# One stretch of scores and one of value products per sequence in a two-layer attention and FFN kernel

## What is computed

```python
h = shift_token(x)
q, k, v = split(h @ wqkv)
q, k = rotary_xpos(l2norm(q) * qs, l2norm(k) * ksc)
x = x + local_attention(q, k, v) @ wo
h = layernorm(shift_token(x)) * lg + lb
a, g = split(h @ w1 + b1)
x = x + (a * gelu(g)) @ w2 + b2
```

## Time and profile before

| | |
|---|---|
| median of 3 runs | 1419.7 us (1419.18 to 1420.46) |
| profiled execution, span | 1416.2 us (3.5 us below the median; its own device time isn't listed) |
| TensorE busy | 1385.3 us |
| VectorE busy | 1090.6 us |
| ScalarE busy | 935.8 us |
| GpSimd busy | 761.9 us |

### The profile page before, as it was taken

The page is one execution under the profiler, slowest core; times in us unless marked ns, Lnnn a source line. Parts: engine busy times, 40 slices in busy tenths (PEclk is TensorE's granted clock), DMA queues, the critical chain, the costliest instruction groups (busy, mean ns, idle before and its releaser), DMA issues.

```text
span 1416.2 us, 32735 instructions
## 1 busy us (share of the span) xinstructions
PE 1385.3 (98%) x11563; PEld 1237.8 (87%) x11563; DVE 1090.6 (77%) x3067; ACT 935.8 (66%) x2662; POOL 761.9 (54%) x576
## 2 busy tenths in 40 slices
PE   8999999989999999999999999999999999999998
PEld 7999998778888888888888888888888888888887
DVE  5777776768788788888888878778778888888874
ACT  6877777456666666666666667666666666666662
POOL 1212222556566566666666667666656666666653
PEclk9999999999999999999999999999999999999999
DMA  5223122101100100010001211111111111111001
GB/s 190 90 92 110 48 67 90 47 20 29 30 30 30 30 29 28 28 28 28 28 29 29 71 29 37 33 35 37 37 37 37 36 36 36 36 36 37 29 30 31
DMA packets 50516, 63.41 MB, mean 45 GB/s; under 512 B 8402, under 2 KB 32104, under 8 KB 50408
## 3 DMA queue, kind: packets, MB, share of 16 engines
q1 hardware_dynamic: 50408, 61.99, 14.0%
HBM read 38.17 MB, written 16.78 MB: 39 GB/s over the span
## 4 chain that ended last, share of the span: by engine, by line
PE 65%; DVE 16%; ACT 9%; issue 5%; DMA 2%; POOL 1%; SPq 1%; DVEq 0%; ACTq 0%; POOLq 0%
PE pb L567 30%; PE pb L880 6%; PE pb L894 6%; PE pb L856 5%; PE pb L825 5%; PE pb L840 5%; ACT x_p L1079 4%; PE pb L920 4%; DVE p_t L1596 2%; DVE p_t L1610 2%; ACT x_pt L1085 2%; DVE r_sin L1583 2%; DVE n_sq L1562 2%; DMA x<-x 1%; DVE r_cos L1577 1%
## 5 line engine op out<-in xcount | busy, mean ns | idle before, releaser
L1823 POOL TENSOR_TENSOR n_inv<-n_cl,half_neg 128x16 f32<-128x16 f32 x64 | 211.2, 3299 | 178.2 <-DVE n_cl L1567 174.7
L1222 ACT ACTIVATE p_t<-p_t,s_nm 128x128 f32<-128x128 f32 (+1 forms) x512 | 227.0, 447 | 22.3 <-DVE s_nm L1596 20.9
L567 PE MATMUL pb<-h_hi,w_hi 128*128 128x256 f32 x704 | 207.5, 295 | 1.3 <-DVE h_lo L1558 1.2
L567 PE MATMUL pb<-h_hi,w_lo 128*128 128x256 f32 x704 | 198.7, 282 | 0.0
L567 PE MATMUL pb<-h_lo,w_hi 128*128 128x256 f32 x704 | 198.6, 282 | 0.0
L1828 POOL TENSOR_TENSOR r_cos<-r_cos,r_sin 128x1024 f32<-128x1024 f32 x64 | 154.6, 2415 | 53.8 <-DVE r_sin L1583 53.8
L1213 ACT ACTIVATE pt_t<-pb 128x512 f32<-128x512 f32 x192 | 114.3, 597 | 98.5 <-PE pb L840 97.8
L1178 ACT ACTIVATE qk_sq<-pb 128x512 f32<-128x512 f32 x128 | 72.5, 592 | 142.9 <-PE pb L567 141.5
L567 PE MATMUL pb<-wqkv_hi,xt_hi 128*128 128x512 f32 x384 | 163.9, 427 | 2.6 <-DVE r_sin L1583 2.3
L1859 POOL TENSOR_TENSOR hg_lo<-hg,hg_hi 128x256 fp32r<-128x256 f32 (+1 forms) x192 | 141.9, 760 | 44.5 <-DVE hg_hi L1627 44.5
L1596 DVE CUSTOM_DVE_ANT_0 p_t<-pb,mask_t 128x128 f32<-128x128 f32 (+1 forms) x512 | 151.9, 353 | 17.5 <-PE pb L825 17.3
(11 more groups left out here) (145 smaller groups left out, 3907.5 us busy)
## 6 DMA issues: line engine op xcount, KB each, us to landing
y_state<-x SPq DMA_DIRECT2D x32, 256.0 KB, 2.0
x_cur<-y_state SPq DMA_DIRECT2D x32, 256.0 KB, 2.6
x_res<-y_state SPq DMA_DIRECT2D x32, 256.0 KB, 2.8
x_in<-x SPq DMA_DIRECT2D x16, 256.0 KB, 2.9
x_state<-x SPq DMA_DIRECT2D x16, 256.0 KB, 2.0
x_orig<-x_state SPq DMA_DIRECT2D x16, 256.0 KB, 2.9
out<-x SPq DMA_DIRECT2D x16, 256.0 KB, 2.2
x<-x SPq DMA_DIRECT2D x32, 112.0 KB, 2.3
```

The costliest lines, as they stand in the source:

```text
L567: mm = pe.matmul(dst, s, m, start=(n == 0 and k == 0), stop=(n == len(pairs) - 1 and k == 2))
L1222: e = nc.scalar.activation(pu, pu, ACT.Exp, bias=s_nm[:, j, k:k + 1], scale=-1.0, accum_out=s_sum[:, j, k:k + 1])
L1823: nc.gpsimd.tensor_tensor(n_inv[:, t], n_cl[:, t], half_neg[:], ALU.pow).then_inc(pool_inv, 1)
```

## The change

The first pair of units now has window 0 (128 keys, four heads each); pairs 1 and 2 have window 1. Each unit has a bank of its own (2, 7, 3, 5, 4, 6), and all three pairs of scores stand at the head of the iteration. Pair 2 waits for the first residual, which reads bank 6; `feed(0)`, which writes bank 7, waits for the maxima of unit 1. All value products of an item are one stretch behind `turn_p(5)`, and wait for all six copies. The copies write into `p_t`, and `pt_t` is gone. On ScalarE `exps(0)` stands ahead of the squares. The orders of VectorE and GpSimd are the same, but unit numbers mean other heads: `maxes`, `exps`, `inverse_sums` and `norm_probs` have four heads of 128 keys in units 0 and 1 and two of 256 keys in units 2 to 5. The core of the diff (the same new arguments at other calls and the idle products of iteration 1 are left out):

```diff
-        pt_t = sb("pt_t", [P, 4, 512], where=L)
...
-        S_BANK = [3, 4, 3, 4, 3, 4]
+        S_BANK = [2, 7, 3, 5, 4, 6]
...
+        def keys_of(u):
+            return P if u < 2 else T
+
         def heads_of(u):
 
-            return range(u // 2 * 4 + u % 2, u // 2 * 4 + 4, 2) if u < 4 else range(u % 2, HEADS, 2)
+            return range(u % 2, HEADS, 2) if u < 2 else range((u // 2 - 1) * 4 + u % 2, u // 2 * 4, 2)
...
                         pe.wait_ge(act_qkt, at(plus(a, -1), 4, 3 if part == 1 else 4))
+                        if part == 2:
+                            pe.wait_ge(dve_max, at(plus(a, -1), UNITS, 1))
...
-                    pe.wait_ge(dve_max, at(b, UNITS, 5))
+                    pe.wait_ge(dve_max, at(b, UNITS, 3))
...
-                        pe.wait_ge(dve_max, at(b, UNITS, UNITS))
+                        pe.wait_ge(dve_max, at(b, UNITS, 5))
...
-            def scores(a, b, j):
+            def scores(a, b, c, j):
 
                 if j == 0:
                         pe.wait_ge(act_qkt, at(b, 4, 4))
+                    if c is not None:
+                        pe.wait_ge(dve_olo, at(c, 2, 2))
+                elif j == 1:
                     if a is not None:
                         pe.wait_ge(act_xhi, at(a, 1, 1))
                         pe.wait_ge(dve_xlo, at(a, 1, 1))
-                else:
-                    pe.wait_ge(dve_max, at(b, UNITS, 2 * j))
-                win1 = j < 2
-                keys = T if win1 else P
-                q_cols = slice(P, T) if win1 else slice(0, P)
+                elif c is not None:
+                    pe.wait_ge(dve_x1, at(c, 1, 1))
+                keys = keys_of(2 * j)
+                q_cols = slice(P, T) if j else slice(0, P)
...
                 pe.wait_ge(dve_pn, at(b, UNITS, u + 1))
+                if u == 0:
+                    pe.wait_ge(dve_max, at(b, UNITS, 4))
...
-            def weigh(b, c, par, j):
-
-                pe.wait_ge(act_pt, at(b, UNITS, 2 * j + 2))
-                if j == 0:
-                    pe.wait_ge(act_v, at(b, NT, NT))
-                    if c is not None:
-                        pe.wait_ge(dve_x1, at(c, 1, 1))
...
+            def weigh(b, c, par):
+
+                pe.wait_ge(act_pt, at(b, UNITS, UNITS))
+                pe.wait_ge(act_v, at(b, NT, NT))
+                pe.wait_ge(dve_max, at(b, UNITS, UNITS))
+                for j in range(3):
+                    for k in range(2 if j else 4):
+                        for t in range(NT if j else 1):
...
-                                           pt_t[:, u % 4, piece * P:piece * P + P],
-                                           start=(t == 0), stop=(t == NT - 1 or j == 2))
+                                               p_t[:, u, piece * P:piece * P + P],
+                                               start=(t == 0), stop=(t == NT - 1 or j == 0))
...
-            def feed(c, d, k):
+            def feed(b, c, d, k):
 
                 if k == 0:
-                    if c is not None:
+                    if b is not None:
+                        pe.wait_ge(dve_max, at(b, UNITS, 2))
+                    elif c is not None:
                         pe.wait_ge(dve_olo, at(c, 2, 2))
...
                 if b is not None:
-                    scores(a, b, 0)
+                    scores(a, b, c, 0)
+                    scores(a, b, c, 1)
+                    scores(a, b, c, 2)
...
-                if b is not None:
-                    scores(a, b, 1)
                 if a is not None and not is_first(a):
                     project(a, d, 0, 2)
...
-                if b is not None:
-                    scores(a, b, 2)
+                if b is not None:
                     turn_p(a, b, d, 0)
...
                 if b is not None:
-                    weigh(b, c, 1 - par, 0)
                     turn_p(a, b, d, 3)
...
                 if b is not None:
                     turn_p(a, b, d, 5)
-                    weigh(b, c, 1 - par, 1)
-                    weigh(b, c, 1 - par, 2)
+                    weigh(b, c, 1 - par)
...
                 act.wait_ge(pe_pt, at(b, UNITS, u + 1))
-                if u == 4:
-                    act.wait_ge(pe_av, at(b, 3, 1))
-                elif u in (0, 2) and later(b):
-                    act.wait_ge(pe_av, at(plus(b, -1), 3, 3 if u == 0 else 2))
-                nc.scalar.activation(pt_t[:, u % 4], pb[:, PT_BANK[u]], ACT.Copy).then_inc(act_pt, 1)
+                nc.scalar.activation(p_t[:, u], pb[:, PT_BANK[u]], ACT.Copy).then_inc(act_pt, 1)
...
+                if b is not None:
+                    exps(b, 0)
                 if a is not None and not is_first(a):
                     square(a, 0, 0)
                     square(a, 0, 1)
                 if b is not None:
-                    exps(b, 0)
                     exps(b, 1)
                     exps(b, 2)
...
                 if later(b):
-                    dve.wait_ge(pe_pt, at(plus(b, -1), UNITS, j + 1))
+                    dve.wait_ge(pe_av, at(plus(b, -1), 1, 1))
```

More of the change, by code:

```diff
@@ L841, in turn_p @@
                 mm.then_inc(pe_pt, 1)
-            def weigh(b, c, par, j):
-                pe.wait_ge(act_pt, at(b, UNITS, 2 * j + 2))
-                if j == 0:
-                    pe.wait_ge(act_v, at(b, NT, NT))
-                    if c is not None:
-                        pe.wait_ge(dve_x1, at(c, 1, 1))
[L850 to L856, removed]
-                                           pt_t[:, u % 4, piece * P:piece * P + P],
-                                           start=(t == 0), stop=(t == NT - 1 or j == 2))
+            def weigh(b, c, par):
[5 more added lines that the diff above has]
+                        for t in range(NT if j else 1):
+                            for u in (2 * j, 2 * j + 1):
+                                h = heads_of(u)[k]
+                                r, col = (h % 2) * DH, (h // 2 % 2) * T + (P if j else 0)
+                                piece = 2 * k + t if j else k
+                                mm = pe.matmul(pb[r:r + DH, 6 + h // 4, col:col + P], v_t[:, par, t, h * DH:h * DH + DH],
+                                               p_t[:, u, piece * P:piece * P + P],
+                                               start=(t == 0), stop=(t == NT - 1 or j == 0))
                 mm.then_inc(pe_av, 1)
-            def feed(c, d, k):
+            def feed(b, c, d, k):
                 if k == 0:
-                    if c is not None:
+                    if b is not None:
+                        pe.wait_ge(dve_max, at(b, UNITS, 2))
+                    elif c is not None:
                         pe.wait_ge(dve_olo, at(c, 2, 2))
@@ L928, in run_l @@
                 if last_norm:
-                    feed(c, d, 0)
-                    feed(c, d, 1)
+                    feed(b, c, d, 0)
+                    feed(b, c, d, 1)
                     turn_h(b, c)
-                    feed(c, d, 2)
-                    feed(c, d, 3)
+                    feed(b, c, d, 2)
+                    feed(b, c, d, 3)
                     hidden(a, b, c, 0)
                     hidden(a, b, c, 1)
-                    feed(c, d, 4)
-                    feed(c, d, FC - 1)
+                    feed(b, c, d, 4)
+                    feed(b, c, d, FC - 1)
                     for m in gate_chunks(c)[2:]:
@@ L956, in run_l @@
                 if d is not None:
-                    feed(c, d, 2)
+                    feed(b, c, d, 2)
                 if isinstance(g, int) and g == 1:
+                    pe.wait_ge(dve_max, 2)
                     idle_products(6, 7)
@@ L970, in run_l @@
                 if d is not None:
-                    feed(c, d, 5)
+                    feed(b, c, d, 5)
                 if last_attention:
@@ L1208, in probs_copy @@
                 act.wait_ge(pe_pt, at(b, UNITS, u + 1))
-                if u == 4:
-                    act.wait_ge(pe_av, at(b, 3, 1))
-                elif u in (0, 2) and later(b):
-                    act.wait_ge(pe_av, at(plus(b, -1), 3, 3 if u == 0 else 2))
-                nc.scalar.activation(pt_t[:, u % 4], pb[:, PT_BANK[u]], ACT.Copy).then_inc(act_pt, 1)
+                nc.scalar.activation(p_t[:, u], pb[:, PT_BANK[u]], ACT.Copy).then_inc(act_pt, 1)
             def exps(b, j):
-                heads = 2 if j < 4 else 4
-                keys = 512 // heads
+                keys = keys_of(j)
+                heads = 512 // keys
                 act.wait_ge(dve_max, at(b, UNITS, j + 1))
@@ L1226, in out_hi @@
             def out_hi(b):
-                act.wait_ge(pe_av, at(b, 3, 3))
+                act.wait_ge(pe_av, at(b, 1, 1))
                 for k in range(2):
@@ L1601, in inverse_sums @@
             def inverse_sums(b, u):
-                heads = 2 if u < 4 else 4
+                heads = 512 // keys_of(u)
                 dve.wait_ge(act_exp, at(b, UNITS, u + 1))
```

2 lines of the change are left out of this document (1 added, 1 removed).

## The result

The changed kernel takes 1490.6 us (1489.4 to 1493.8, four runs) against 1419.4 for the kernel before in the same set of runs: a ratio of 1.0512, with a 95% interval of 1.0494 to 1.0530 (ratios here and below are estimates over the single runs, so they can differ a little from the quotient of the two medians, here 1.050). It is 71.2 us slower; 74.1 had been forecast.

What follows compares the result with a forecast made beforehand. TensorE bounds the layers with VectorE close behind. Period 35.30 + 0.85 (late sixth turn) + 0.76 (copy wait) + 0.86 (moved values) = 37.77; 2.47 x 30 = 74.1 on 1419.7 gives 1493.8 us, 8-in-10 range 1464 to 1518.

Steps and rivals of the forecast that it cites:

- TensorE's saving, 1.1 us a period: Three of six score and value stretches go on TensorE, each worth about 0.37 us: 1.1 us an iteration.
- the 34.13 of the estimate: Period in us if TensorE's saved switches were all that changed, against 35.30.
- Steps 1 to 3: Iteration head: three score stretches take 2.78 us, rotate 0 starts at 7.09 (was 5.45), rotate 1 at 19.29 (was 18.56).
- the prediction's first rival (12%): VectorE's waits absorb the late rotate 0, only values are late: period 36.92, 1468 us; chance 12%.
- step 3: VectorE's queue from rotate 0 to rotate 1 shrinks from 13.11 to 12.2 us, so rotate 1 starts at 19.29.
- Steps 5 and 6: GpSimd's add_parts ends at 24.61, the second clamp gets through only then, and `turn_p(5)` starts 0.85 us late.
- the prediction's cross-check: Period without stalls, 34.13, plus TensorE's stalls 0.4 + 0.5 + 0.4 + 1.0 + 0.5 + 0.8, is 37.7 us.
- the two cannot run together: VectorE's second clamp and GpSimd's simultaneous instruction exclude each other; the clamp, 1.60 us before, is again held to its end.
- Step 7: Values wait for unit 5's copy, starting 1.35 us after the turn, not 0.59; 48 instructions instead of 32 follow.
- the moved products (0.86): 16 more value instructions stand behind the sixth turn on TensorE: 0.86 us more a period.
- the case that gave 1513: ScalarE's table load costs about 2.66 us and waits for the first maxes; squares start 0.65 late, sum near 1513.
- the rival, in which it falls in each period: Values and two hidden chunks run at the lower clock, 5.7 us doubled each period: near 1665 us; chance 1%.

Runs made afterwards that it cites:

- Experiment 2: Changed kernel with the second and third pairs of scores back in their old places: 1462.9 us, ratio 1.0323 to the kernel before.
- experiment 9: Changed kernel with all engines' orders refitted, and ScalarE copying next x and tile 1's values ahead of turned unit 4: 1400.2 us, ratio 0.9862 to the kernel before.
- A: The changed kernel itself, against the kernel before: 1490.6 us, ratio 1.0512.
- Experiment 4: Changed kernel with VectorE's maxima of units 2 and 3 ahead of the first rotation: 1488.7 us, ratio 1.0491 to the kernel before.
- experiment 6: Changed kernel with GpSimd's add_parts of tile 1 waiting until VectorE has normalised unit 5: 1476.1 us, ratio 1.0398 to the kernel before.
- experiment 5: Changed kernel with unit 5 normalised ahead of VectorE's second clamp: 1491.0 us, ratio 1.0506 to the kernel before.
- experiment 1: Changed kernel with value products starting after four copies, waiting for the sixth only ahead of units 4 and 5: 1469.8 us, ratio 1.0361 to the kernel before.
- experiment 3: Changed kernel with later score pairs back in their old places and values started after four copies: 1442.6 us, ratio 1.0162 to the kernel before.

## Why the prediction was right

- *What bounds.* That TensorE at 98% and VectorE have next to no slack between them was the reading that decided. Experiment 2 shows it from one side (more switches of TensorE, 28 us faster), experiment 9 from the other (the same merged stretches, with the queues fitted, 18 us faster than before).
- *TensorE's saving, 1.1 us a period.* The size is an estimate that no run isolates. Part of it stands in the rows: three stretches of scores took 1.06 each before and take 2.82 together. It showed in the time only once the waits were gone (experiment 9): beside the 34.13 of the estimate, A stands still for 3.8 us of its 37.90.
- *Steps 1 to 3, the head and VectorE's queue.* Confirmed within 0.07 us each. The price of the head in the whole is what experiment 2 gave back, 28 us; the prediction's first rival (12%), in which VectorE absorbs it, is out. Experiment 4 shows a limit of the method: step 3 counted the queue as a sum and was right only since the order beside GpSimd's add_parts stayed as it was.
- *Steps 5 and 6, GpSimd.* The hold came at 24.72 as walked, and experiment 6 priced it at 15 us, that is 0.5 us a period, the 0.5 that the prediction's cross-check has ahead of turn 5. Whether the clamp or something else was held was left open by "the two cannot run together"; experiment 5 settles that it is not the clamp's own doing.
- *Step 7, the values.* The wait (0.76 forecast) gave 20.8 us back in experiment 1, 0.69 a period; the moved products (0.86) are what experiment 3 leaves: 0.84 in its iteration, 23.8 us in the whole, of which 17.5 lie in the thirty periods.
- *The sum.* 74.1 was 3 us too much, and it came this near because errors of opposite sign met. The step that is off is the last: 2.47 times 30 took one iteration's difference for all. The pattern iteration went from 35.30 to 37.90, which is 2.60 and a little more than the 2.47 that was walked. But the thirty of the kernel before averaged 35.56, since some, mainly around and behind the change of layers, had waits of their own; afterwards the thirty average 37.86, so most of these waits disappeared into the new ones. The average rose by 2.30, in all 69.1 of the 70.6 more in the span.
- *The chances.* They add up to 92% for slower and not 91%, since the lower clock is a slower case too.
- *The table load.* It starts right after the copies of q and k without waiting for the maxima (596.92, ahead of the head), so it lies in idle time and the case that gave 1513 did not come.
- *The clock.* Over the thirty iterations the granted clock was 1.00 on average, so the rival, in which it falls in each period, is out. It did fall once, in iteration 2, where a wait was longer than the 1.0 that the prediction allowed:

```profile
304.30 0.62 PE L569 MATMUL pb<-wqkv_hi,xt_hi 128*128 128x512 f32 x1 [2.29 <-DVE r_sin L1587]
304.72 0.63 PE L569 MATMUL pb<-wqkv_lo,xt_hi 128*128 128x512 f32 x1
```

```profile
294.73:332.51 37.78, 32.81 (x255) 28.25 (x254) 27.59 (x80) 22.62 (x61) 21.30 (x15) 0.95 0.07 18
```

Behind 2.29 us of waiting, six products start 0.42 us apart where 0.23 is usual, and the granted clock of that iteration is 0.95. Its period of 37.78 is no longer than the others', so in A it cost nothing that can be seen.

## What to carry to other kernels

When an engine's work is collected into longer stretches, ask what stood between the pieces: it was cover for other engines' latency, and their first inputs now come later by the length of what was moved ahead of them. With in-order queues the merged stretches paid only once the other engines' orders were fitted to them: the same stretches made the kernel 5.1% slower alone and 1.4% faster with four queues reordered. Follow every queue that leads to the late step, GpSimd's too: work taken from VectorE behind the first clamp did not bring turn 5 forward. And before moving a VectorE step, look at what GpSimd does beside it: the steps here that read PSUM could stand there, some of those on SBUF alone were held to the end of GpSimd's instruction.

## What the runs showed of the hardware

- The normalising step of VectorE, with two SBUF inputs, waited beside a large GpSimd `tensor_tensor` (1.9 to 2.8 us on 128 x 1024) for its end: 1.79, 2.18, 2.27 and 2.69 us for a step of 0.69. The clamp, with one SBUF input of 128 x 16, waited too: 1.76 us in A, 0.16 in experiment 5. Not every step on SBUF does: the sums of squares, which read one SBUF array of 128 x 1024, took 1.20 to 1.22 us in all twelve traces, with GpSimd at work beside them or idle, and the inverse sums were never held (0.13 to 0.18 for one). The steps that read PSUM were never held either. Beside add_parts in A (VectorE, then GpSimd):

```profile
608.33 1.22 DVE L1566 TENSOR_REDUCE n_sq<-qk_sq 128x16 f32<-128x1024 f32 x1
```

```profile
607.12 2.42 POOL L1832 TENSOR_TENSOR r_cos<-r_cos,r_sin 128x1024 f32<-128x1024 f32 x1 [3.11 <-DVE r_sin L1587]
```

- Beside GpSimd's power on 128 x 16 (3.3 us), VectorE steps on SBUF were not held. In A, GpSimd's power ran from 614.48 to 617.78, and VectorE in that time:

```profile
615.02 0.43 DVE L1557 CAST h_hi<-h_n 128x512 fp32r<-128x512 f32 x1
615.48 0.69 DVE L1562 TENSOR_TENSOR h_lo<-h_n,h_hi 128x512 fp32r<-128x512 f32 x1
```

- Score products with 128 and with 256 keys follow each other in one stretch without a gap: 2.82 us for 32 instructions, against 1.06 for a single stretch of 8, so two exits (0.36 together) are gone.
